# The last stage of a two-layer attention and feed-forward kernel: its first loads on ScalarE's queue, POOL's own wait, statistics by tile, later steps for the second batch, fewer unread products

## The reference

```
X  = X + sum_k w8[k] * y_rows[slot8[k]]          # 8 experts' rows for each token
q  = layernorm(X)                                 # "n"
s  = q @ ctx.T / sqrt(512), masked                # "s", "sc"
X  = X + softmax(s) @ ctx                         # "e", "r", "x"
h  = layernorm(X)                                 # "n4_", "x4T"
out = X + ds * ((silu(gs * (h @ Wg)) * us * (h @ Wu)) @ Wd)
```

## Time and profile before

| | us |
|---|---|
| median of 3 runs | 1505.08 (1503.83 to 1509.4) |
| the profiled execution, its own time | 1498.16 |
| its span in the trace | 1496.4 |
| TensorE busy in the span | 1405.8 (94%) |
| VectorE, ScalarE, POOL busy | 1036.4 (69%), 877.0 (59%), 627.3 (42%) |

### The profile page before, as it was taken

One profiled execution on the slowest core, in us unless ns is written; L12 is line 12 of the kernel. 1 busy time (PEld: TensorE's weight loads), 2 busy tenths in 40 slices (PEclk: granted clock), 3 DMA queues, 4 the chain that ended last, 5 costly groups with the idle time before them and its releaser, 6 DMA issues.

```text
span 1496.4 us, 39189 instructions
## 1 busy us (share of the span) xinstructions
PE 1405.8 (94%) x8784; PEld 1194.8 (80%) x8785; DVE 1036.4 (69%) x2209; ACT 877.0 (59%) x2138; POOL 627.3 (42%) x727
## 2 busy tenths in 40 slices
PE   7999999999846999999999999999997899999998
PEld 5887766667625889888988998898885788888888
DVE  5555699976687777767777767667666666776732
ACT  5555699973356666666666766666652444344442
POOL 1222488861156222322333323222254766776322
PEclk9999999999955999999999999999998899999999
DMA  6221594001162788888778877778775745444100
GB/s 232 85 85 57 193 366 160 2 5 57 57 260 66 266 272 298 270 272 277 263 265 271 287 269 256 257 255 269 262 227 175 247 148 155 154 151 130 56 21 23
DMA packets 93134, 277.77 MB, mean 186 GB/s; under 512 B 12725, under 2 KB 12854, under 8 KB 92342
## 3 DMA queue, kind: packets, MB, share of 16 engines
q1 hardware_dynamic: 45910, 156.67, 30.5%
q0 software_dynamic: 23520, 77.09, 17.2%
q10 hardware_dynamic: 23616, 43.00, 7.7%
HBM read 208.55 MB, written 76.81 MB: 191 GB/s over the span
## 4 chain that ended last, share of the span: by engine, by line
PE 34%; issue 12%; DMA 5%; POOL 5%; ACTq 4%; ACT 4%; DVE 3%; DVEq 1%; SPq 0%; POOLq 0%
PE m_g L1400 14%; PE m_y L1420 8%; PE f_g L1894 5%; DMA y_rows<-y 4%; POOL G L1767 2%; POOL hT_low L1773 2%; PE f_y L1909 2%; PE m_x L1385 2%; ACT y L1601 1%; ACTq L1231 1%; ACTq L1605 1%; DMA raw_d<-in_exp_d 1%; PE f_sc L1848 1%; DVE X L1946 1%; ACT wgu_high L1121 1%
## 5 line engine op out<-in xcount | busy, mean ns | idle before, releaser
L1294 POOL DMA_INDIRECT xg<-h_rows,idx x160 | 163.2, 1020 | 431.6 <-PE m_x L1385 421.0
L1400 PE MATMUL m_g<-wgu_high,bxTh 128*128 x660 | 236.4, 358 | 6.8 <-DVE bxTl L1473 6.3
L1400 PE MATMUL m_g<-wgu_low,bxTh 128*128 x660 | 223.0, 338 | 0.0
L1400 PE MATMUL m_g<-wgu_high,bxTl 128*128 x660 | 222.9, 338 | 0.0
L1894 PE MATMUL f_g<-x4T_high,ffn_gu 128*128 128x256 f32 x704 | 176.9, 292 | 6.2 <-DVE x4T_low L2016 6.2
L1133 DVE TENSOR_TENSOR wgu_low<-raw_gu,wgu_high (+1 forms) x128 | 122.5, 959 | 86.8 <-ACT wgu_high L1121 66.7
L1894 PE MATMUL f_g<-x4T_low,ffn_gu 128*128 128x256 f32 x704 | 170.2, 283 | 0.0
L1121 ACT ACTIVATE wgu_high<-raw_gu (+1 forms) x128 | 108.0, 846 | 75.2 <-issue 73.8
L1420 PE MATMUL m_y<-wd_high,hidTm 128*128 x328 | 139.5, 425 | 5.7 <-issue 3.2
L1894 PEld LDWEIGHTS f_g<-x4T_high,ffn_gu 128*128 128x128 f32 x704 | 135.1, 192 | 11.8 <-issue 10.4
L657 POOL TENSOR_TENSOR prob<-prob,inv 128x512 f32<-128x512 f32 x128 | 130.6, 1042 | 24.8 <-DVE inv L603 23.0
(11 more groups left out here) (292 smaller groups left out, 3341.6 us busy)
## 6 DMA issues: line engine op xcount, KB each, us to landing
raw_gu<-in_exp_gu SPq DMA_DIRECT2D x64, 768.0 KB, 6.7
y_rows<-y ACTq DMA_DIRECT2D x164, 256.0 KB
raw_d<-in_exp_d SPq DMA_DIRECT2D x64, 512.0 KB, 7.5
y_rows<-zero SPq DMA_DIRECT2D x64, 256.0 KB, 3.4
ffn_gu<-ffn_gu_words SPq DMA_DIRECT2D x1, 5632.0 KB, 23.7
raw_c<-in_ctxT SPq DMA_DIRECT2D x16, 256.0 KB, 2.6
X<-in_x SPq DMA_DIRECT2D x4, 1024.0 KB, 5.5
h_rows<-h SPq DMA_DIRECT2D x16, 256.0 KB, 2.0
```

Source lines behind the costliest of these rows:

```text
L1294: eng.indirect_dma_start(xg[:, u, :].bitcast(F32), None, h_dram, bass.IndirectOffsetOnAxis(ap=idx[half][:, u:u + 1], axis=0)).then_inc(s_g ...
L1400: m = eng.matmul(pg[u % 2][:, 0:2 * I], xT[l][:, u % 2, c, :], W.gu[r][:, buf * DC + c, :], start=c == 0 and n == 0, stop=c == DC - 1 and ...
```

## The change

- The first three loads of the last stage (`memT`, the mask, `mem`) move from SP's order to ScalarE's, behind its last store.
- POOL waits for the last stores itself, not for SP's `s_over`; it makes 12 gathers ahead of `deviations_4(0)` instead of 14, and 5 behind it, where it made 11 and `deviations_a(1)`. The rest is taken from one list in order by `gather_next`; batch 0 has one gather beside each f and three at f = 6 (`GATHERS_0`), with two more and `deviations_a(1)` at f = 3, and leaves eight of batch 3 to the batches behind it.
- `read_in` is made by tile: add, statistics, aggregation of tile 0, then of tile 1.
- Ahead of batch 0 ten adds of batch 1 are left of sixteen; six stand beside f = 0 to 2 of batch 0, `moments_a(1)` at f = 2 and `scales_a(1)` and `norm_3(1)` at f = 3.
- In batch 0 the second batch's steps stand at f = 6, 7, 9, 10 on PE, where they stood at 3, 4, 6, 8; at 5, 6, 9, 10 on DVE with `scales_4` behind the loop; at 5, 6, 8 on ACT.
- `low(1)` stands ahead of `store(0, 0)`.
- `keep_clock(8)` becomes 7, and a second one 6. An unused SiLU (`silu_first`) stands behind `high_4(0)`. `negatives(0)` stands ahead of `valid`.

```diff
@@ -1656,7 +1657,8 @@
     ADDS = {0: 2, 1: 3, 2: 2, 3: 1, 4: 1, 8: 1}
     GATHERS = {1: 1, 2: 2, 3: 1, 4: 1, 5: 1, 6: 1, 7: 1}
 
-    GATHERS_2, GATHERS_3 = {0: 2, 1: 2, 2: 2, 3: 1}, {4: 1, 5: 1, 6: 1, 7: 1, 8: 1, 9: 1, 10: 2}
+    GATHERS_0, GATHERS_1 = {f: 3 if f == 6 else 1 for f in fs}, {0: 1, 1: 2, 2: 1, 3: 1, 4: 2, 5: 1, 6: 1, 7: 1}
+    FIRST_ADDS, ADDS_0 = {0: (10, 12), 1: (12, 14), 2: (14, 16)}, {4: 2, 5: 2, 7: 2, 8: 2, 9: 1}
     with ExitStack() as held_here:
         sb = lambda name, shape, dt=F32: held_here.enter_context(nc.sbuf_tensor(name, shape, dt))
         ps = lambda name, shape, dt=F32: held_here.enter_context(nc.psum_tensor(name, shape, dt))
@@ -1672,6 +1674,7 @@
         score, nmax, tot, inv = sb("score", [P, TPB, S]), sb("nmax", [P, TPB, 2]), sb("mtot", [P, TPB]), sb("minv", [P, TPB])
         prT = sb("mpT", [P, TPB, TPB, P])
         ones, minus_half = sb("f_ones", [P, 1]), sb("minus_half", [P, TPB])
+        silu_first = sb("silu_first", [P, 1])
         Wdn = sb("ffn_d", [P, FC, D], F32R)
         hT = [sb(f"hT_{h}", [P, FC, S], F32R) for h in ("high", "low")]
         G = sb("G", [P, TPB, K, D])
@@ -1691,7 +1694,7 @@
         peC = Steps(nc, ctx, "f_peC", each("x3T", "s", "pT", "r", "x4T"))
         peG, peY = Steps(nc, ctx, "f_peG", [f"g{f}" for f in fs]), Steps(nc, ctx, "f_peY", each("y"))
         dveA = Steps(nc, ctx, "f_dveA", [f"k{k}_{i}" for k in range(K) for i in TI] + each("st", "mv") + ["shift"])
-        dveC = Steps(nc, ctx, "f_dveC", ["neg"] + each("sc", "max", "nmax", "inv", "invv", "x", "st4", "mv4") + ["shift4"] + each("x4Tl"))
+        dveC = Steps(nc, ctx, "f_dveC", ["neg"] + each("sc", "max", "nmax", "inv", "invv") + [n + str(i) for i in TI for n in ("x", "st4", "mv4")] + ["shift4"] + each("x4Tl"))
         dveH = Steps(nc, ctx, "f_dveH", [f"h{f}" for f in fs])
         dveY = Steps(nc, ctx, "f_dveY", [n for i in TI for n in (f"s{i}", f"o{i}")])
         actC = Steps(nc, ctx, "f_actC", each("n", "x3T", "e", "pT") + each("n4_", "x4Th"))
@@ -1718,11 +1721,6 @@
                 eng.dma_start(mem[:, :, :], a["mem"][:, bass.ts(b, TPB), :]).then_inc(s_mem, 16)
 
             groups = used_groups(eng, endb)
-            added.wait(eng, 0, f"k{K - 1}_{TPB - 1}")
-            apart(eng, s_apart)
-            load_T(0)
-            eng.dma_start(open8[:, :, :], a["mask"].unsqueeze(0).to_broadcast([P, B, S])).then_inc(s_m, 16)
-            load(0)
             for u in range(2):
                 eng.wait_ge(s_y[u], groups * 32 + 16)
             eng.sem_inc(s_over, 1)
@@ -1786,36 +1784,42 @@
             def deviations_4(b):
                 deviations(b, poolR4, dveC, "4", mv4, lnp4)
 
+            groups = used_groups(eng, endb)
             added.wait(eng, 0, f"k{K - 1}_{TPB - 1}")
             apart(eng, s_apart)
             Chain(nc, ctx, "f_poolc", eng)(eng.memset(minus_half[:, :], -0.5))
             deviations_a(0)
-            eng.wait_ge(s_over, 1)
-            gather(1, places[:14])
+            for u in range(2):
+                eng.wait_ge(s_y[u], groups * 32 + 16)
+            apart(eng, s_apart)
+            gather(1, places[:12])
             deviations_4(0)
-            gather(1, places[14:])
-            gather(2, places[:4])
-            deviations_a(1)
-            gather(2, places[4:9])
-
+            gather(1, places[12:])
+
+            rows = deque((b, place) for b in range(2, B) for place in places)
+
+            def gather_next(last, n):
+                for _ in range(n):
+                    if rows and rows[0][0] <= last:
+                        b, place = rows.popleft()
+                        gather(b, [place])
+
+            gather_next(2, 1)
             for b in range(B):
-                n, of_2, beside = 0, 9, GATHERS if b > 0 else GATHERS_3
+                beside = GATHERS_0 if b == 0 else GATHERS_1 if b < 3 else GATHERS
                 for f in fs:
+                    if b == 0 and f == 3:
+                        deviations_a(1)
+                        gather_next(2, 2)
                     low(b, f)
-                    if b == 0:
-                        gather(2, places[of_2:of_2 + GATHERS_2.get(f, 0)])
-                        of_2 += GATHERS_2.get(f, 0)
-                    if b < B - 1 and f == 7 + 2 * (b == 0):
+                    gather_next(b + 3 if b > 0 else 2, beside.get(f, 0))
+                    if b < B - 1 and f == (10 if b == 0 else 7):
                         deviations_4(b + 1)
-                    if b < B - 3:
-                        gather(b + 3, places[n:n + beside.get(f, 0)])
-                        n += beside.get(f, 0)
-                if b < B - 3:
-                    gather(b + 3, places[n:n + 4])
+                gather_next(b + 2, 2 * K)
+                gather_next(b + 3, 4)
                 if b < B - 2:
                     deviations_a(b + 2)
-                if b < B - 3:
-                    gather(b + 3, places[n + 4:])
+                gather_next(b + 3, 4)
 
         @block.tensor
         def _(eng):
@@ -1864,7 +1868,7 @@
                     peC.done(m, f"r{i}")
 
             added.wait(eng, 0, f"k{K - 1}_0")
-            keep_clock(8)
+            keep_clock(7)
             turn(0, "x3T", "n")
             scores(0)
             keep_clock(3)
@@ -1872,7 +1876,7 @@
             read(0)
             eng.wait_ge(s_odd, 1)
             eng.matmul(py[0][0:1, 0:1], odd[:, :], ones[:, :], start=True, stop=True).then_inc(s_sum, 1)
-            keep_clock(8)
+            keep_clock(6)
             eng.wait_ge(s_exact, 1)
             apart(eng, s_apart)
             all_exact = eng.value_load(exact[0:1, 0:1], min_val=0, max_val=1)
@@ -1880,10 +1884,11 @@
             keep_clock(2)
 
             def gate_up(b, more, way, late):
-                beside = {1: lambda: turn(b + 1, "x3T", "n"), 2: lambda: scores(b + 1), 4: lambda: turn_probs(b + 1), 6: lambda: read(b + 1)}
+                steps = (lambda: turn(b + 1, "x3T", "n"), lambda: scores(b + 1), lambda: turn_probs(b + 1), lambda: read(b + 1))
+                beside = dict(zip((6, 7, 9, 10) if late else (1, 2, 4, 6), steps))
                 for f in fs:
-                    if more and f - late in beside:
-                        beside[f - late]()
+                    if more and f in beside:
+                        beside[f]()
                     if f < GUB:
                         dveH.wait(eng, b - 1, f"h{[x for x in fs if x % GUB == f][-1]}")
                     else:
@@ -1992,19 +1997,24 @@
                     dveC.wait(eng, b, f"inv{i}")
                     dveC.done(eng.tensor_tensor(inv[:, i:i + 1], inv[:, i:i + 1], valid[:, bass.ds(b, 1)], ALU.mult), f"invv{i}")
 
-            def add_read(b):
-                for i in TI:
-                    dveC.wait(eng, b, f"invv{i}")
-                    peC.wait(eng, b, f"r{i}")
-                    t = b * TPB + i
-                    dveC.done(eng.scalar_tensor_tensor(X[:, t, :], px[i][:, :], inv[:, i:i + 1], X[:, t, :], ALU.mult, ALU.add), f"x{i}")
-
-            def read_in(b):
+            def read_in(b, i):
+                dveC.wait(eng, b, f"invv{i}")
+                peC.wait(eng, b, f"r{i}")
+                t = b * TPB + i
+                dveC.done(eng.scalar_tensor_tensor(X[:, t, :], px[i][:, :], inv[:, i:i + 1], X[:, t, :], ALU.mult, ALU.add), f"x{i}")
+                dveC.wait(eng, b, f"x{i}")
+                apart(eng, s_apart)
+                dveC.done(eng.bn_stats(stats4[:, i, :], X[:, t, :]), f"st4{i}")
+                dveC.wait(eng, b, f"st4{i}")
+                apart(eng, s_apart)
+                dveC.done(eng.bn_aggr(mv4[:, i, :], stats4[:, i, :]), f"mv4{i}")
+
+            def read_in_0(b):
                 inverses(b)
-                add_read(b)
-
-            def moments_4(b):
-                moments(b, dveC, "4", "x{}", dveC, stats4, mv4)
+                read_in(b, 0)
+
+            def read_in_1(b):
+                read_in(b, 1)
 
             def scales_4(b):
                 scales(b, dveC, poolR4, "4", mv4, lnp4)
@@ -2048,26 +2058,25 @@
             moments_a(0)
             scales_a(0)
             eng.wait_ge(s_m, 16)
+            negatives(0)
             link(eng.tensor_reduce(valid[:, :], open8[:, :, :], axis=AX.X, op=ALU.max))
-            negatives(0)
             maxima(0)
             eng.wait_ge(s_over, 1)
             link(eng.memset(ones[:, :], 1.0))
             find_odd()
-            add(1, adds[:4])
-            read_in(0)
-            moments_4(0)
+            add(1, adds[:3])
+            read_in_0(0)
+            read_in_1(0)
             find_exact()
+            add(1, adds[3:4])
             scales_4(0)
-            add(1, adds[4:10])
+            add(1, adds[4:6])
             low(0)
-            add(1, adds[10:])
-            moments_a(1)
-            scales_a(1)
+            add(1, adds[6:10])
             eng.wait_ge(s_s, 48)
 
             def one(b, more, more2, late=0):
```

(41 more changed lines are left out.)

## The result

The changed kernel takes **1515.2 us** (median of 7 runs, 1509.21 to 1518.14), the kernel before 1507.49 beside it: ratio 1.0039, 95% interval 1.0020 to 1.0058. It is a little slower; 1492.8 was predicted, with a chance of 0.05 for slower, and the range ended at 1499. Two repeats gave 1.0056 (1.0037 to 1.0076) and 1.0028 (1.0010 to 1.0046). Its profiled execution took 1517.26 us, span 1515.5.

What follows compares the result with a forecast made beforehand. It took the last stage's start, a chain of small steps, and an overlong batch 0 as what costs time. Terms 7.6 + 4.4 + 0.5 - 0.2 = 12.3 us off 1505.1 gave 1492.8, range 1486 to 1499.

Steps and rivals of the forecast that it cites:

- the eight gathers put off: Batches 1, 2 and 5: gathers left by batch 0 cost nothing in POOL's idle time, up to 1.5 us otherwise; 0.2 taken.
- 0.5 gained in batch 1: Batch 1: its norm comes 0.3 us earlier and some of POOL's lateness goes, 0.5 us gained in all.
- Statistics by tile: Stage's start, behind the second read: tile 0's statistics done while TensorE works on tile 1, a gain of 0.4 us.
- The start: Last stage up to batch 0's first gate/up product: earlier loads, scores, maxima and low part begin batch 0 7.6 us earlier.
- The idle time of 3.01 us is gone, so I take full clock: Scores at the stage's start: without the wait for `memT` they take 3.6 us instead of 6.7.
- 5.9 and 0.4: Stage's start: 5.9 us gained up to the maxima, 0.4 by statistics by tile, with the turn put 6.05 us earlier.
- the sum of stalls: Batch 0: TensorE's waits of 1.4, 0.9, 0.5, 0.6 and 1.8 us, 5.2 us in all.
- the walk: Batch 0, step by step: 39.8 us of work and 5.2 of stalls, some 45.1 us, 4.4 less than 49.5.
- both stretches at low clock are gone: Batch 0: given, with POOL's 17 gathers ahead and eight left for later, as the reason for its gain of 4.4 us.
- The two rules: Skill rules weighed: a drain of about 1.38 us behind each table load, and a clock falling at times the program does not choose.
- The early table load: ScalarE ahead of batch 0: SiLU's table loads under the low part, 1.29 us off the first SiLU, off the path.
- falls and stays: Rival, batch 0: more idle time ahead of it leaves its eleven f and scores at 1.2 GHz, 1514.0 us; chance 0.05.

Runs made afterwards that it cites:

- e1: Kernel after with POOL's deviations_4 ahead of the gather of f = 7 again in batches 1 to 6; ratio 1.0000 to the kernel before.
- e3: Kernel after with batches 1 and 2 using the later batches' list of gathers, two more in each moving to batch 5; ratio 1.0003 to the kernel before.
- e5: Kernel after with root ahead of gather, both tiles' statistics together and the old gather list in batches 1 and 2; ratio 0.9978 to the kernel before.
- e2: Kernel after with both adds first, then both tiles' statistics, as before, in every batch; ratio 1.0045 to the kernel before.
- r1_again: Kernel after run once more, unaltered; ratio 1.0056 to the kernel before.
- r2_again: Kernel after run once more, unaltered, on the chip of a repeat of the kernel before; ratio 1.0028 to the kernel before.
- b_again: Kernel before run once more, unaltered; ratio 1.0004.

## Why the prediction was wrong

- **The later batches: the step that failed.** It was "the eight gathers put off ... nothing if they fall into POOL's idle time ... I take 0.2", with 0.5 gained in batch 1, and with no term at all for the order inside POOL's loop and for the statistics by tile in batches 1 to 6. Measured: +10.9. I read POOL's busy time (29.55 of 42.47) as room. But POOL's work between f = 6 and f = 8 is on a chain: statistics, root, shift, `h9`, low part, down products. A gather of 1.2 us ahead of the root is 1.2 us on that chain (e1). Two gathers more in each of batches 1 and 2 make POOL's low parts late there (e3: 4.6 in the two batches, some of it low clock, 1.15 given back in batch 5). With the three causes undone (e5), 0.7 is gained in batch 1 (0.5 said) and 0.8 lost in batch 5 (0.2 said, 1.5 the bound). By the diff alone the swap of `gather_next` and `deviations_4` was to be seen; I costed the edit only in batch 0, where the root moved to f = 10.
- **Statistics by tile** were costed once, at the start (a gain of 0.4). They are in every batch, where each instruction now waits 0.15 us for the one before it: 0.2 to 0.95 us each in batches 3 to 5 (e2). The gain at the start is hardly there either: e2, with both tiles together, and e3, by tile, both with a fast read, turn the rows for batch 0 at +22.74 and +22.60 and begin it at 25.5 and 25.6.
- **The start** was mis-sized: 5.3 instead of 7.6. Loads, scores and maxima came as worked out, within 0.4. "The idle time of 3.01 us is gone, so I take full clock" was right for the scores and wrong behind them. Where the read ran in 3.70 us (e2, e3) the start was 25.5 and 25.6, 0.9 from my 24.65; where it ran in 5.40 (r1_again, r2_again, e1) it was 26.9 to 27.2. The low clock is worth the 1.5 us between. And 3.0 of the gain was read from one execution: in b_again the scores of the kernel before were fast already. The sum has a small slip too: 5.9 and 0.4 make the turn 6.3 earlier, not 6.05.
- **Batch 0**: the sum of stalls was right, in part by luck, and the gain was not. TensorE's idle time in the three profiles after is 4.9 us each (5.2 in the walk). The turn of f = 6 waits 1.90 (walked 1.4), the read nothing (0.9), the down products 0.67 (0.5), the next turn 0.64 (0.6), the end 1.28 (1.8). But before's idle time was 4.6, 3.7 and 5.0: as much stood there all along, in other places. All of my gain was that "both stretches at low clock are gone". They are not: mean clock 0.93, 0.96, 0.95 after, 0.90, 0.91, 0.97 before. At half clock a share 2 x (1 - mean clock) of the batch runs, and half of it is lost: (1 - 0.947) x 48.2 = 2.6 us after, by the same sum 3.5 before, an estimate. I compared one execution that had 9.9 us of low clock in batch 0 with a walk that had none.
- **The two rules.** The early table load did what its row said: the table and a small activation fill ScalarE's time under the low part, and the first SiLU came behind the first f, as taken (no run leaves the early load out, so its gain is not measured). The drain of 1.38 us of the Trainium skill (ScalarE: Activation LUTs, What ACT_TABLE_LOAD costs) is not to be found in the start either: the load ran from 1174.93 for 1.28 us, the small SiLU began at 1176.22. On the clock, the read ran slow (5.40) with the scores at full clock ahead of it, and fast (3.70) in e2 and e3 with the same code up to there and the same 0.75 us of idle time ahead of it as in r1_again: the Trainium skill (TensorE: Matmul & The Clock Gate, Part 1) says that it falls at times which the program does not choose, and the traces agree. The rival "falls and stays" did not come; what came is that it fell elsewhere.
- I named what would prove me wrong: batches 1 and 2 growing by over 1 us each. They grew by 2.9 to 3.7 and by 3.0 to 3.8.

**Open**: the pauses of 3.6 to 6 us in the start on one chip, in both kernels; what sets the clock at batch 0's first f; and why the low clock fell on the scores in two of three profiles of the kernel before and on the read in all three after.

## What to carry to other kernels

Cost an edit in every iteration of the loop that it stands in, not only where it was meant to act: an order swapped by one place cost some 1.2 us in each of four batches and ate the gain of the stage's start. Busy time is no measure of room on an engine that has a link of a chain in its queue; ask which instructions may stand ahead of that link. And do not book low clock as recoverable: take it out of both sides of the comparison first, by several profiles if need be.
